# Attention kernel: the weighed sum issued in two halves per step, and the maxima turned by VectorE

## The reference

```python
q = x @ q_w.T + q_b                                  # 16 heads of 16
xd = conv1d(x, conv_w, stride=2, pad=1) + conv_b     # per channel: 2048 -> 1024 rows
k, v = xd @ k_w.T + k_b, xd @ v_w.T + v_b
att = softmax(einsum('bhnd,bhmd->bhnm', q, k) * 0.25)
x = layernorm(x + (att @ v) @ out_w.T + out_b)
h = layernorm(x) * gamma + beta
x = layernorm(x + x + 0.5 * (silu(h @ w1 + b1) @ w2 + b2))   # w1, w2 dequantised from integers
```

## Time and profile before

| | |
|---|---|
| median of 3 runs | 3911.18 us (3905.49 to 3913.1) |
| the profiled execution | span 3912.8 us, its own time; the median is 1.6 us below it |
| attention, first to last copy-out of `pv_ps` | 300.5 to 3021.1 us |
| busy share of the span | TensorE 98%, weight loads 51%, VectorE 85%, ScalarE 67%, GpSimd 22% |
| mean granted TensorE clock | 0.985 of full speed |

### The profile page before, as it was taken

One profiled execution on the slowest core, in us unless ns is written; L12 is line 12 of the kernel. 1 busy time (PEld: TensorE's weight loads), 2 busy tenths in 40 slices (PEclk: granted clock), 3 DMA queues, 4 the chain that ended last, 5 costly groups with the idle time before them and its releaser, 6 DMA issues. The chain is left out here.

```text
span 3912.8 us, 76603 instructions
## 1 busy us (share of the span) xinstructions
PE 3836.0 (98%) x22744; PEld 1996.5 (51%) x22744; DVE 3334.3 (85%) x4142; ACT 2612.8 (67%) x4969; POOL 844.9 (22%) x553
## 2 busy tenths in 40 slices
PE   8979999999999999999999999999999999999998
PEld 5643333333333333333333333333334899999998
DVE  9979998999899899989989998999996777777775
ACT  4428887888788788878878887888887334343343
POOL 6522100000000000000000000000001787787775
PEclk9979999999999999999999999999999999999999
DMA  8991133115103311510231051024111222222220
GB/s 295 345 201 58 50 48 56 33 34 70 34 27 49 56 33 34 70 34 27 47 57 34 29 68 38 30 46 59 33 36 58 78 85 83 67 86 78 72 86 27
DMA packets 315388, 269.34 MB, mean 69 GB/s; under 512 B 156593, under 2 KB 225201, under 8 KB 315314
## 3 DMA queue, kind: packets, MB, share of 16 engines
q1 hardware_dynamic: 314194, 264.36, 27.6%
q0 software_dynamic: 1120, 4.19, 0.4%
HBM read 157.30 MB, written 110.10 MB: 68 GB/s over the span
## 5 line engine op out<-in xcount | busy, mean ns | idle before, releaser
L751 DVE TENSOR_REDUCE half_max<-first_ps 128x2 f32<-128x1024 f32 x2038 | 2402.0, 1221 | 280.1 <-PE first_ps L590 276.1
L717 ACT ACTIVATE probs<-score_ps 128x512 f32<-128x512 f32 x4096 | 2114.7, 603 | 578.4 <-PE score_ps L615 577.8
L615 PE MATMUL score_ps<-q_s,k_s 49*128 49x512 f32 x4096 | 1444.2, 477 | 23.5 <-DMA q_s<-max_row 12.8
L615 PEld LDWEIGHTS score_ps<-q_s,k_s 49*128 49x128 f32 x4096 | 574.6, 185 | 1284.4 <-ACT probs L717 1156.1
L625 PE MATMUL pv_ps<-probs,v_s 128*32 128x512 f32 x8192 | 1102.2, 610 | 0.0
L590 PE MATMUL first_ps<-k_s,q_s 48*128 48x512 f32 x4076 | 903.3, 421 | 14.2 <-PEq L189 9.5
L860 POOL TENSOR_TENSOR num<-num,rden 128x1024 f32<-128x1024 f32 x2 | 4.7, 2373 | 2585.3 <-DMA rden<-rden_d 2585.3
L1035 ACT ACTIVATE act_f<-fc_ps,b 128x512 f32<-128x512 f32 x256 | 174.9, 684 | 470.4 <-PE fc_ps L988 468.3
L590 PEld LDWEIGHTS first_ps<-k_s,q_s 48*128 48x128 f32 x4076 | 408.6, 188 | 61.5 <-issue 10.9
L1112 DVE CAST a_hi<-act_f 128x512 fp32r<-128x512 f32 x256 | 241.9, 946 | 146.6 <-ACT act_f L1035 146.0
L1164 POOL TENSOR_TENSOR a_lo<-act_f,a_hi 128x512 fp32r<-128x512 f32 x256 | 339.4, 1331 | 86.1 <-DVE a_hi L1112 86.1
(11 more groups left out here) (109 smaller groups left out, 2540.0 us busy)
## 6 DMA issues: line engine op xcount, KB each, us to landing
q_s<-q_hi_d SPq DMA_DIRECT2D x512, 64.0 KB, 2.1
o_d<-o_sb SPq DMA_DIRECT2D x128, 256.0 KB, 2.1
x_t<-x_c_in SPq DMA_DIRECT2D x32, 512.0 KB, 5.8
q_hi_d<-q_hi SPq DMA_DIRECT2D x32, 512.0 KB, 4.8
q_lo_d<-q_lo SPq DMA_DIRECT2D x32, 512.0 KB, 5.1
k_s<-k_hi_d SPq DMA_DIRECT2D x128, 128.0 KB, 4.3
q_s<-q_lo_d SPq DMA_DIRECT2D x256, 64.0 KB, 2.1
x_res<-x_in SPq DMA_DIRECT2D x32, 512.0 KB
```

The source lines that it names most:

```text
L615: pe.matmul(bank(s, u)[:, :], k_s[g][at, a, t * P:(t + 1) * P], q_s[g][at, a, :], start=True, stop=True).then_inc(scored, 1)
L717: nc.scalar.activation(probs[s % 2][:, u, :], bank(s, u)[:, :], ACT.Exp).then_inc(exped, 1)
L751: dve.reduce_max(half_max[g % 2][:, :, a * TT + t, keys], first_ps[keys][:, :, :], AX.X)\
```

## The change

The weighing is issued in two halves of 256 queries. The new order of a step is S S F F half, S S F F half, with S a score and F a first product. The turn moves from TensorE to VectorE, which transposes in squares of 32x32; `neg_max` grows to 32 columns (16 stay zero), and `max_row` becomes 128x32: in each 32 partitions, 16 rows with the maxima of 32 queries. Each of these squares goes into `q_s` by transfers of its own, so `load_max` issues 4 x 2 = 8 transfers for 2, and `m_loaded` counts 128 a group for 32. The ring is shifted no more.

```diff
-        neg_max = [sb(f"neg_max{i}", [P, TT * HG]) for i in two]
-        max_row = [sb(f"max_row{i}", [TT * HG, P], F32R) for i in two]
+        SQ = 32
+        neg_max = [sb(f"neg_max{i}", [P, SQ], F32R) for i in two]
+        max_row = [sb(f"max_row{i}", [P, SQ]) for i in two]
-        QL, KVL, ML, OS = 6 * 16, 7 * 16, 2 * 16, 16
+        QL, KVL, ML, OS = 6 * 16, 7 * 16, 2 * (P // SQ) * 16, 16
-        AFTER = TURN + 2
+        SKIP = 1
         def bank(s, u):
-            return score_ps[(4 * s + u + (s - AFTER + KT) // KT) % RING]
+            return score_ps[(4 * s + u) % RING]
...
                     row = q_s[g][at:at + 1, :, :].rearrange("p a (t q) -> p (a t) q", t=TT)
-                    sp.dma_start(row.bitcast(F32), max_row[g % 2][h * 2 * TT:(h + 1) * 2 * TT, :].bitcast(F32))\
-                        .then_inc(m_loaded[g], 16)
+                    for k in range(P // SQ):
+                        square = max_row[g % 2][k * SQ + h * 2 * TT:k * SQ + (h + 1) * 2 * TT, :]
+                        sp.dma_start(row[:, :, k * SQ:(k + 1) * SQ].bitcast(F32), square).then_inc(m_loaded[g], 16)
...
-            def turn_max(n, s):
...
-            def score(n, s, u, more):
-                n, s = (n + 1, 0) if s == STEPS else (n, s)
+            def score(n, s, u):
+                n, s = (n + 1, s - STEPS) if s >= STEPS else (n, s)
                 if t == 0 and u == 0:
                     pe.wait_ge(m_loaded[g], 1 + ML * (n + 1))
-                behind_turn = t == AFTER
-                if behind_turn and u == 2 and (more or s + KT - 2 < STEPS):
-                    pe.wait_ge(row_up, 1 + G * n + g + 2)
-                near = behind_turn and u < 2
-                pe.wait_ge(exped, 4 * (STEPS * n + s) + u + 1 + near)
+                skipped = SKIP if s == 0 and u < RING - SKIP else 0
+                pe.wait_ge(exped, 4 * (STEPS * n + s) + u + 1 + skipped)
...
-            def weigh(n, s):
+            def weigh(n, s, part):
-                if t == 0:
-                    pe.wait_ge(o_up, 1 + G * n + g)
-                pe.wait_ge(exped, 4 * (STEPS * n + s + 1) + RING)
+                if part == 0:
+                    if t == 0:
+                        pe.wait_ge(o_up, 1 + G * n + g)
+                    pe.wait_ge(exped, 4 * (STEPS * n + s + 1) + RING)
+                queries = slice(part * QB // 2, (part + 1) * QB // 2)
                 for h in range(HG):
-                    last = pe.matmul(pv_ps[h * VC:(h + 1) * VC, :], v_s[g][:, t, h, :], probs[s % 2][:, h, :],
-                                     start=t == 0, stop=t == KT - 1)
-                last.then_inc(pv_done, 1)
+                    last = pe.matmul(pv_ps[h * VC:(h + 1) * VC, queries], v_s[g][:, t, h, :], probs[s % 2][:, h, queries],
+                                     start=t == 0 and part == 0, stop=t == KT - 1, skip_group_check=True)
+                if part == 1:
+                    last.then_inc(pv_done, 1)
...
-                    if follow:
-                        score(n, s + 1, 0, more)
-                        score(n, s + 1, 1, more)
-                    if ahead:
-                        first(n, s + LEAD, 0)
-                        first(n, s + LEAD, 1)
...
-                    weigh(n, s)
-                    if s % KT == TURN and (more or s + KT < STEPS):
-                        turn_max(n, s)
+                    for part in range(2):
+                        if follow:
+                            score(n, s + 1, 2 * part)
+                            score(n, s + 1, 2 * part + 1)
+                        if ahead:
+                            first(n, s + LEAD, 2 * part)
+                            first(n, s + LEAD, 2 * part + 1)
+                        else:
+                            again(s, part)
+                        weigh(n, s, part)
...
                 dve.wait_ge(m_loaded[slot], 1 + ML * full)
-                dve.wait_ge(turned, G * n + g + 1)
-                dve.tensor_copy(max_row[g % 2][:, :], bank(s + 1, 4)[0:TT * HG, 0:P]).then_inc(row_up, 1)
+                dve.wait_ge(maxed, G * n + g + 1)
+                dve.transpose(max_row[g % 2][:, :], neg_max[g % 2][:, :].bitcast(F32)).then_inc(row_up, 1)
```

More of the change, by code:

```diff
@@ L484, in attention @@
         o_stored = [sem(f"o_stored{i}") for i in two]
-        maxed, turned, row_up = (sem(n) for n in ("maxed", "max_turned", "row_up"))
+        maxed, blank, row_up = (sem(n) for n in ("maxed", "neg_max_blank", "row_up"))
         scored, exped, pv_done, o_up = (sem(n) for n in ("scored", "exped", "pv_done", "o_up"))
@@ L496, in attention @@
         TURN = (2 * KT - LEAD) % KT
-        AFTER = TURN + 2
+        SKIP = 1
         def bank(s, u):
-            return score_ps[(4 * s + u + (s - AFTER + KT) // KT) % RING]
-        assert (4 * STEPS + G) % RING == 0
+            return score_ps[(4 * s + u) % RING]
+        assert (4 * STEPS + SKIP) % RING == 0
         block = ctx.enter_context(nc.Block())
@@ L698, in _ @@
                     first(0, part, u)
[L699 to L702, removed]
+            for u in range(HG):
+                score(0, 0, u)
             with pe.Fori(0, NB - 1) as n:
@@ L755, in maxima @@
                     halves = half_max[g % 2][:, :, :, :].rearrange("p h c k -> p (h c) k")
-                    dve.tensor_reduce(neg_max[g % 2][:, :], halves, AX.X, ALU.max, negate=True)\
+                    dve.tensor_reduce(neg_max[g % 2][:, 0:TT * HG], halves, AX.X, ALU.max, negate=True)\
                         .then_inc(maxed, 1)
@@ L781, in one_block @@
                         rows(n, s)
+            for i in two:
+                dve.memset(neg_max[i][:, :].bitcast(F32), 0.0).then_inc(blank, 1)
+            dve.wait_ge(blank, 2)
             for part in range(EARLY, LEAD):
```

## The result

The changed kernel takes 4950.5 us (median of 4 runs, 4934.2 to 4962.4) against 3911.2: 1.266 times as long, 95% interval 1.263 to 1.269. The sign was forecast; the size was not, since 4950 lies above the range's 4690. The profiled execution took 4958.0 us with a span of 4956.2.

A forecast was written before the change was run, and what follows sets the result against it. A loop through TensorE and ScalarE bound the kernel, VectorE close below. 127 groups of 26.1 us (23.0 cycle with eight transfers, 3.1 low clock) less 2720.6 gave +594, late queue +14: 4520 us, range 4130 to 4690.

The forecast's parts named there:

- The step: Attention step on TensorE: two half steps of 0.34 + 0.33 + 0.55 = 1.22 us, 2.44 against 2.61.
- rival 3: In the step, each half weighing costs the whole 0.99 us; step 3.32, group 27.4, 4670 us; chance 0.04.
- The wait for the copy-out: At a group's start, the next group's first half weighing waits 0.3 us for ScalarE's copy of `pv_ps`.
- The transfers: SP's eight transfers of the maxima: spacing 0.72 us, turn to score 7.25, TensorE standing still 3.1 us per group.
- rival 2: On SP's queue, eight transfers are no longer than two; all hidden at 0.27 us spacing, 3735 us; chance 0.08.
- A stall brings the clock down: On TensorE, a 3.1 us stall in every group drops the clock to 1.2 GHz in every group.
- rival 1: At TensorE's stalls, the queue binds but the clock stays up; group 23.0 us, 4140 us; chance 0.11.
- How long it stays down: TensorE's low clock behind each stall: 7.4 us on average, at a loss of 0.42, 3.1 us per group.
- Stall and clock: In each group's cycle, TensorE's 3.1 us stall and 3.1 us low-clock loss add, giving 26.1 us.
- The instructions: The step's eight extra matmuls and loads on TensorE were counted within the half step's 1.22 us.
- The top of the range: Upper limit for the whole kernel's time: a group of 27.4 us, 4690 us.
- The worst case that the prediction named for the clock: TensorE's clock down 10.2 us each time at a loss of 0.5: group 28.1 us, some 4780 us.

The follow-up runs named there:

- the pair above: Changed kernel with four transfers and the turn a step earlier, halves only in groups 2 and 3 (3858.8 us) or only in groups 0 and 1 (3905.3 us).

## Why the prediction was wrong, point by point

- **The step** was forecast at 2.44 us and is 2.48. A half weighing leads to the next pair after 0.57 us (1320.18 to 1320.75), forecast at 0.55: rival 3 is out. The wait for the copy-out is 0.33 us for 0.3.
- **The transfers**: spacing 0.69 us for 0.72, turn to score 6.83 for 7.25, the transpose 0.20 for 0.27. Rival 2 is out, and the eight transfers in the kernel before show the queue, with its spells, to be worth +13%. A quarter of the bytes left the issue time where it was (635 ns for 647). The section of the Trainium skill that rival 2 took the small cost of descriptors from describes transfers issued by GpSimd; these are issued on SP. The spacing at which that rival's cycle equals today's 21.2 us is 0.46 us, not 0.48 (15.75 + 0.3 + 1.91 + 7 x 0.46); nothing else rests on it.
- **A stall brings the clock down**: right, and rival 1 is out. Of 104 gaps of 1.5 us or more between matmul starts that began at full clock, 98 were followed by the lower one.
- **How long it stays down** is the step that failed. "44.3 us together", "7.4 on average" was measured behind the old order and carried over to the new one. Behind the new order a spell lasts 21.6 us on average. I counted 127 x 3.1 = 394 us for it; 2092 us low, less 81 in which TensorE stood still anyway, at a loss of 1 - 2.48/4.32 = 0.43 are some 860. The loss rate, 0.42, was right.
- **Stall and clock** were two costs that add in my sum, and they do not: at the lower clock TensorE reaches the score after the transfers have landed, and nine groups took 8 x 4.32 = 34.6 us with no stall. So the waits came to 276 us (268.0, and 8.3 on the weight loads) instead of 394. Together, 860 - 394 = 466 more for the clock, 118 less for the waits and 119 for the branches make 467, near the miss of 430; these parts overlap in places.
- **The instructions** were priced by their time in the array alone ("the eight extra matmuls and loads of a step are in the 1.22"). They also lengthen the loop body: 25 of 31 branches took over 1 us, 119 us in all. Ten of these began at full clock, and each was followed by a fall within 6 us; the other 15 began when it was already low. No part of the prediction had this.
- **The top of the range**, 4690 us, came from rival 3, and so from another cause than the one at work. The worst case that the prediction named for the clock (4780 us) took 10.2 us per spell, the longest of six, all behind the same order.

What stays open is which property of the order in halves keeps the clock low, and why some spells behind it are short all the same. It is not the size of the matmuls (halves back to back: 6.4 us) and not the number of instructions (the pair above). It may be the doubled passages between row halves and column strips or the spacing of the work (4.32 us a step at the lower clock, 4.07 before); no run separates these.

## What to carry to other kernels

Before one transfer is cut into several on one queue, multiply the issue time by their number and hold it against the slack from its trigger to its first use, here 4.98 us against 5.4 of issue alone. A price taken from a trace holds only for the work around it: the length of a clock spell belonged to the order of the work behind the stall. And a faster schedule is worth most where nothing stalls: halves in the groups that follow no late transfer, in a loop body that is short enough, come out 1.3% under the kernel before (3858.8 us, 0.987), where halves everywhere with eight transfers cost 27%. Halves in group 1 as well gained no more (3856.1 us).

## What the runs showed of the hardware that I had not expected

- A TensorE that is busy without a gap stayed at 1.2 GHz for 47.8 us under one order of matmuls (halves in groups 0 and 1; in the changed kernel 64.9 us, with gaps of up to 1.8 us), and came back within 3.4 to 17.1 us under another (108 spells: the kernel before, with two transfers and with eight).
- The branch at the end of TensorE's loop over blocks takes 0.2 us or 4 to 5 us. I count some 1240 instructions of TensorE per pass in the kernel before and 1740 in the changed one; with 128 fewer than that it is 0.2 us, so for these loops the border lies between 1610 and 1740. The packets on the instruction queue rose from 22 to 251 with it, and are 25 with halves in three groups. The Trainium skill (Runtime: NRT & Kernel Launch, Instruction fetch mechanics) says that a taken branch whose target is not in the current window of two pages forces a fetch of the target before execution goes on; it gives pages of 256 instructions and room for 2048 on TensorE. The trace agrees on the fetch, with 4777 ns and the packets. Neither two pages nor 2048 instructions is the border here: bodies of up to 1610 branched back in 0.2 us, and 1740 did not.
- A transfer of 16 rows into two partitions takes 500 ns to issue, one of 8 rows into one 635.
